# LSTM step on one core: two column groups of the fifth gate ahead of the wait for the state's second half, and an output gate and a tanh that change memories

## The reference

```python
def step(carry, xp):
    h, c = carry
    gates = xp + h @ W_hh.T
    i, f, g, o = jnp.split(gates, 4, axis=-1)
    c = jax.nn.sigmoid(f) * c + jax.nn.sigmoid(i) * jnp.tanh(g)
    h = jax.nn.sigmoid(o) * jnp.tanh(c)
    return ((h, c), h)
_, hs = jax.lax.scan(step, (h0, c0), jnp.swapaxes(x_proj, 0, 1))
```

## Time and profile before

| | us |
|---|---|
| runs | 14405.98, 14417.92, 14417.6 |
| median | 14417.6 |
| span of the profiled execution, first to last instruction | 14425.7 |
| first to last L1510 weight load | 3964.9 to 14307.1 |

### The profile page before, as it was taken

One profiled execution on the slowest core, in us unless ns is written; L12 is line 12 of the kernel. 1 busy time (PEld: TensorE's weight loads), 2 busy tenths in 40 slices (PEclk: granted clock), 3 DMA queues, 4 the chain that ended last, 5 costly groups with the idle time before them and its releaser, 6 DMA issues. The chain is left out here.

```text
span 14425.7 us, 1970254 instructions
## 1 busy us (share of the span) xinstructions
PE 12650.9 (88%) x904808; PEld 11223.3 (78%) x904808; DVE 6842.5 (47%) x48363; ACT 6802.9 (47%) x42405; POOL 2877.4 (20%) x4598
## 2 busy tenths in 40 slices
PE   3697878878699999999999999999999999999998
PEld 2585766756588888888888888888888888888886
DVE  5868677775533333333333333333333333333335
ACT  2474655655144444444444444444444444444443
POOL 5675757667000000000000000000000000000000
PEclk7898998988899999999999999999999999999998
DMA  4454545545200000000000000000000000000000
GB/s 91 128 152 120 148 128 143 136 129 145 94 3 3 2 2 2 3 2 2 2 3 2 2 3 2 2 3 3 2 2 2 3 2 2 3 2 2 3 2 20
DMA packets 692140, 542.16 MB, mean 38 GB/s; under 512 B 545207, under 2 KB 595929, under 8 KB 679740
## 3 DMA queue, kind: packets, MB, share of 16 engines
q1 hardware_dynamic: 469456, 315.98, 8.8%
q0 software_dynamic: 221600, 223.50, 6.6%
q10 hardware_dynamic: 934, 0.99, 0.0%
HBM read 286.02 MB, written 252.14 MB: 37 GB/s over the span
## 5 line engine op out<-in xcount | busy, mean ns | idle before, releaser
L1510 PE MATMUL p_g<-ring,wh 128*32 128x16 f32 x800000 | 8099.8, 185 | 663.2 <-DVE ring L1613 401.0
L1510 PEld LDWEIGHTS p_g<-ring,wh 128*32 128x32 f32 x800000 | 7487.6, 109 | 1438.2 <-DVE ring L1613 1134.2
L1551 ACT ACTIVATE cell<-p_g 128x3 f32<-128x3 f32 x12500 | 2180.9, 174 | 5594.6 <-PE p_g L1510 5594.6
L1606 DVE CUSTOM_DVE_ANT_1 cj<-cell 128x4 f32<-128x4 f32 x12500 | 2038.6, 163 | 5732.3 <-ACT cell L1551 5732.3
L1648 POOL COPY hist<-ring 128x6 f32 x2501 | 475.3, 190 | 10239.6 <-POOLq L1647 10239.6
L426 POOL DMA_INDIRECT eb<-node_tab,eidx x1650 | 2128.2, 1290 | 1013.6 <-POOLq L424 587.6
L1484 PE MATMUL p_g<-xq,idn 128*32 128x24 f32 (+3 forms) x80032 | 1614.8, 189 | 61.6 <-PEq L1497 15.3
L1484 PEld LDWEIGHTS p_g<-xq,idn 128*32 128x32 f32 x80032 | 1254.7, 110 | 231.6 <-issue 15.5
L1613 DVE SCALAR_TENSOR_TENSOR ring<-og,p_g 128x1 f32<-128x1 f32 x6250 | 969.1, 155 | 631.9 <-ACT p_g L1555 1.8
L1555 ACT ACTIVATE tc<-cell 128x1 f32<-128x1 f32 x6250 | 1219.9, 195 | 0.0
L1555 ACT ACTIVATE p_g<-cell 128x1 f32<-128x1 f32 x6250 | 1089.4, 174 | 0.0
(11 more groups left out here) (224 smaller groups left out, 7731.8 us busy)
## 6 DMA issues: line engine op xcount, KB each, us to landing
edge_tab<-eb SPq DMA_DIRECT2D x98, 1019.8 KB
edge_tab<-eb SPq DMA_DIRECT2D x96, 566.6 KB
edge_tab<-eb SPq DMA_DIRECT2D x96, 339.9 KB
eb<-node_tab,eidx POOLq DMA_INDIRECT x1650
xp_tab<-xo SPq DMA_DIRECT2D x50, 500.0 KB, 2.6
xq<-xp_tab SPq DMA_DIRECT2D x1251, 8.0 KB, 1.7
xq<-xp_tab SPq DMA_DIRECT2D x1250, 12.0 KB, 1.7
edge_tab<-eb SPq DMA_DIRECT2D x98, 118.4 KB
```

The costliest lines, as they stand in the source:

```text
L1510: m = pe.matmul(to[32 * q:32 * q + 32], wh[:, k, D * q + 32 * c:D * q + 32 * c + 32], ring[:, (s - 1) % TS, k:k + 1].broadcast_to([128, w] ...
L1551: act.activation(cell[:, s, k, 0:6:2], gate_at(h, u, k)[:, :, 0], ACT.Tanh).then_inc(l_s[k], 1)
L1606: dve.tensor_tensor_reduce(cj[:, k, :].rearrange("p (a b) -> p a b", a=2), cell[:, s, k, 0:4].rearrange("p (a b) -> p a b", a=2), cell[:, ...
```

## The change

Three things: `gate` takes a list of quads, and two of the four groups of column 4 with k = 0 go ahead of the wait for ring's second half; the groups of columns 0 to 2 with k = 1 behind the wait run in the order of quads 2, 3, 0, 1, and the other two groups of column 4 follow them. Half 0's output gate goes to SBUF (`og`, now with an index k), and its tanh of c to PSUM, in scratch columns of bank 0 instead of bank 2. So both halves now have the output gate in SBUF and the tanh in PSUM.

```diff
--- before.py
+++ after.py
@@ -1408,7 +1408,7 @@
                 xq = [sb(sub, f"xq{h}", [128, HB[h], GT]) for h in range(2)]
                 ring = sb(sub, "ring", [128, TS, KC])
                 cell = sb(sub, "cell", [128, TS, KC, 6])
-                og, tc = sb(sub, "og", [128, 2]), sb(sub, "tc", [128, 2])
+                og, tc = sb(sub, "og", [128, KC, 2]), sb(sub, "tc", [128, 2])
                 cj = sb(sub, "cj", [128, KC, 4])
                 part_of = ((0, 3), (3, 6), (6, 7), (7, 8))
                 p_g = [[ps(sub, f"p_g{h}{n}") for n in range(4)] for h in range(2)]
@@ -1440,7 +1440,7 @@
 
                 def late_at(h, u, k):
 
-                    return p_g[h][2 + k][:, 504 + u:505 + u]
+                    return p_g[h][3 * k][:, 504 + u:505 + u]
 
                 @block.sync
                 def _(sp):
@@ -1503,10 +1503,10 @@
                             h, u = place(s)
                             g, v = turn(s)
 
-                            def gate(c, k, w=W):
+                            def gate(c, k, quads=(0, 1, 2, 3), w=W):
                                 n = c // 3 if c < 6 else c - 4
                                 to = gate_at(h, u, n)[:, c - part_of[n][0], 0:w]
-                                for q in range(4):
+                                for q in quads:
                                     m = pe.matmul(to[32 * q:32 * q + 32],
                                                   wh[:, k, D * q + 32 * c:D * q + 32 * c + 32],
                                                   ring[:, (s - 1) % TS, k:k + 1].broadcast_to([128, w]), start=False, stop=(k == KC - 1), skip_group_check=True)
@@ -1514,12 +1514,13 @@
                             pe.wait_ge(l_h[g][0], v)
                             for c in (0, 1, 2, 3):
                                 gate(c, 0)
+                            gate(4, 0, (0, 1))
                             pe.wait_ge(l_h[g][1], v)
                             for c in (0, 1, 2):
-                                m = gate(c, 1)
+                                m = gate(c, 1, (2, 3, 0, 1))
                             m.then_inc(l_g[0], 1)
-                            for c in (4, 5):
-                                gate(c, 0)
+                            gate(4, 0, (2, 3))
+                            gate(5, 0)
                             for c in (3, 4, 5):
                                 m = gate(c, 1)
                             m.then_inc(l_g[1], 1)
@@ -1551,12 +1552,10 @@
                                 act.activation(cell[:, s, k, 0:6:2], gate_at(h, u, k)[:, :, 0], ACT.Tanh).then_inc(l_s[k], 1)
 
                             def tanh_c(k):
-                                to = late_at(h, u, 1) if k else tc[:, s % 2:s % 2 + 1]
-                                return act.activation(to, cell[:, (s + 1) % TS, k, 5:6], ACT.Tanh)
+                                return act.activation(late_at(h, u, k), cell[:, (s + 1) % TS, k, 5:6], ACT.Tanh)
 
                             def out_gate(k):
-                                to = og[:, s % 2:s % 2 + 1] if k else late_at(h, u, 0)
-                                return act.activation(to, gate_at(h, u, 2 + k)[:, :, 0], ACT.Tanh)
+                                return act.activation(og[:, k, s % 2:s % 2 + 1], gate_at(h, u, 2 + k)[:, :, 0], ACT.Tanh)
                             act.wait_ge(l_g[0], s + 1)
                             gates(0)
                             act.wait_ge(l_g[1], s + 1)
@@ -1609,8 +1608,7 @@
                                                          0.5, 0.0, ALU.mult, ALU.add, cell[:, (s + 1) % TS, k, 5:6]).then_inc(l_c[k], 1)
 
                             def new_h(k):
-                                gate, th = (og[:, s % 2:s % 2 + 1], late_at(h, u, 1)) if k else (late_at(h, u, 0), tc[:, s % 2:s % 2 + 1])
-                                dve.scalar_tensor_tensor(ring[:, s, k:k + 1], gate, 1.0, th,
+                                dve.scalar_tensor_tensor(ring[:, s, k:k + 1], og[:, k, s % 2:s % 2 + 1], 1.0, late_at(h, u, k),
                                                          ALU.add, ALU.mult).then_inc(l_h[turn((s + 1) % TS)[0]][k], 1)
                             dve.wait_ge(l_s[0], s + 1)
                             new_c(0)
```

## The result

The changed kernel takes 14537.0 us (median of 4 runs, 14533.4 to 14539.1); the kernel before, in runs on the same chip, 14415.6 us (4 runs, 14406.0 to 14417.9). The ratio is 1.0085, with a 95% interval of 1.0073 to 1.0098: slower by 121 us, where 14555 us and +137 us had been forecast. The profiled execution took 14539.1 us, its span is 14537.3, against 14425.7.

The account below looks back on a forecast made before the run. The first half's loop (TensorE to gates(1), tanh_c(0), out_gate(0), new_h(0), next load) was taken to bound the step. Terms 18 + 8 - 4 = +22 ns over 6250 steps gave 137.5 us, so 14555 us; range 14412 to 14595.

Parts of the forecast that it names:

- The views and the loop: Step of 1.65 us closed by the first half: TensorE to gates(1), then tanh_c(0), out_gate(0), new_h(0), next load.
- Term 5: Second half: gates(1), new_c(1), tanh_c(1) stay in place, new_h(1) stays at 1.70 us and gains slack.
- The wait is free: TensorE's wait for ring's second half opens just as reached and costs nothing; moving two groups ahead fills no hole.
- The stall rival: TensorE idles up to 33 ns at the second-half wait, so the change runs faster: -12 ns a step, 14343 us; 9%.
- Term 1: Two groups moved ahead of l_g0 put gates(0) 33 ns later, at 0.755 us; gates(1) stays at 1.08.
- The rotation at nothing: Rotated group order on TensorE keeps consecutive groups on different columns, so it was costed at zero.
- Term 2: l_c0 opens later, a cover of 15 ns is used up, and tanh_c(0) starts 18 ns late; bounds 10 to 25.
- Term 3: tanh_c(0) to PSUM: the interval to out_gate(0) stays 0.09 us, going with what the first operation reads.
- Term 4: out_gate(0) to SBUF takes 171 instead of 163 ns, +8 on the path; new_h(0) then -4.
- new_h(0) −4: new_h(0) takes the form of new_h(1): 155 instead of 159 ns, -4 a step.
- fixed overlap: ScalarE overlap stays 0.10 us, so out_gate(0) starts 0.072 behind tanh_c(0): 0 to +4 ns, some 14424 us; 18%.
- A write that must land: tanh_c(0)'s PSUM write must finish before out_gate(0) reads PSUM: +103 ns a step, 15060 us; 6%.

Follow-up runs that it names:

- the wait one group earlier: Kernel before, with 15 instead of 16 groups ahead of the wait for ring's second half and the order rotated to match: 14449.4 us, ratio 1.003.
- four groups: Kernel before, with all four groups of gate 4's first pass ahead of the wait, memories as before: 14772.4 us, ratio 1.0244.
- one-group kernel: Kernel before, with one column group of gate 4 instead of two ahead of the wait, memories as before: 14463.4 us, ratio 1.003.
- groups only: Kernel before, with only TensorE's group order as in the change (two groups ahead of the wait, rotated), memories as before: 14562.3 us, ratio 1.0101.
- after: The changed kernel, with both the group order and the two memories changed against the kernel before: 14537.0 us, ratio 1.0085.
- memories only: Kernel before, with only tanh_c(0) moved to PSUM and out_gate(0) to SBUF, TensorE's order as before: 14424.1 us, ratio 1.0004.
- The one run that was to hold tanh_c(0) back: Kernel with four groups ahead of the wait, plus an unread ACTIVATE between gates(1) and tanh_c(0): 14805.2 us, ratio 1.0274.

## Why the prediction was right, and which of its terms were not

The direction, the place and the size held: forecast +22 ns a step and 14555 us, measured +20 and 14537. Point by point:

- *The views and the loop.* Right. The loop of the first half sets the step: in every kernel here the next load stands 53 ns behind new_h(0)'s end (before: 1599.7 and 1652.9). Term 5 holds too: new_h(1) starts at 1700.3, before at 1700.5, and only with the wait one group earlier does the second half hold TensorE by more than it catches up (gates(1) 7.9 ns late).
- *The wait is free.* Right. gates(1) did not move, the burst has the same 38 loads in 0.30 us, and an earlier wait shows about 9 ns of slack. "The wait has next to no slack" was roughly right too, only that a hole of that size is filled again within four loads. The stall rival is refuted.
- *Term 1, 33 ns at gates(0).* Measured 34.0; one, two and four groups give 16.6, 33.3 and 66.6. *The rotation at nothing:* right, and it is worth 17 ns in the run without it.
- *Term 2, +18 ns from a cover of 15.* The start of tanh_c(0) moved by 18.0 (1169.7 against 1151.7), exact as a statement on that start. What it left out is that the cover on the path is not that of tanh_c(0)'s start: out_gate(0)'s start moved by 34.4, its end by 24.4 (1408.1 to 1432.5). The one-group kernel parts the three: 2.4 ns at tanh_c(0)'s start, 18.8 at out_gate(0)'s start, 9 at its end.
- *Term 3, the interval stays 0.09.* Failed: 109 ns, +16. The source of the data, which I took as what decides, is the same in both, and the destination doesn't decide either: 109 with SBUF (groups only) and with PSUM (after), 93 with SBUF (before) and with PSUM (memories only; there the opening + 109 comes to the same time, so this pair says only that it isn't longer). What decides is whether l_c0 or the queue is last. The trace of before held a hint, outside my groups. ScalarE's timeline of the kernel before, at two places where it comes from idling:

```profile
2869.46 0.20 ACT L878 ACTIVATE kf<-kd 128x2 f32<-128x2 f32 x1 [2.21 <-ACTq L877]
2869.57 0.45 ACT L880 ACTIVATE x<-p,kn 128x250 f32<-128x250 f32 x1
...
3535.84 0.21 ACT L1207 ACTIVATE c<-c 125x10 f32<-125x10 f32 x1 [30.90 <-DVE c L1262]
3535.96 0.20 ACT L1208 ACTIVATE c<-c 125x10 f32<-125x10 f32 x1
3536.06 0.39 ACT L1209 ACTIVATE wgt<-mm,cn 125x125 f32<-125x125 f32 x1
```

  The pair whose 0.09 I took as my upper bound stands here again, behind 2.21 us of idle time, and the interval is 0.11. In the second piece the one behind the idle time has 0.12 and its follower 0.10. At both places the interval behind the operation that had to wait is the longer one: 0.11 against the 0.09 of the earlier trace rows, 0.12 against 0.10.
- *Term 4, out_gate(0) 171 instead of 163.* Failed: 154, −10 instead of +8. I took the duration of out_gate(1) for a property of the two memories. Of PSUM to SBUF the runs show 171, 168 and 154 ns, of PSUM to PSUM 164 and 153: it is 153 to 154 with either destination where l_c0 holds it clearly (after, and one, two and four groups). *new_h(0) −4:* right, 155.
- *The two errors cancel.* From the start of tanh_c(0) to the end of out_gate(0) I had 93 + 171 = 264 ns, and it is 109 + 154 = 263. Terms 2, 3, 4 as measured: 18 + 16 − 10 − 4 = +20. That the total came out within 2 ns is luck in these two. The forecast lengthened this way from 256 to 264 for a write to SBUF. As measured, the memories alone take it from 256 to 261, l_c0 alone to 262.5, and both together to 262.8.
- *The halves don't add.* Groups alone cost 144 us, memories alone 6 (not told from none), together 121. Behind an l_c0 that is late, out_gate(0) takes 153 or 154 ns in either memory, so the cost of SBUF for it is gone, and new_h(0)'s 158 to 155 remains as a gain: with the memories the two-group step is 1.6726, without them 1.6752.
- *The rivals.* The fixed overlap is refuted by the result beside the groups alone: behind 174 ns and behind 203 ns out_gate(0) comes 109 later, overlaps of 65 and 94. With the memories alone the overlap is 76, and in the kernel before 102, so no two of these kernels share one. My own reading, that the source sets the interval, was an estimate from a few intervals, and it falls with this one: with tanh_c(0) reading `cell` every time, the interval is 93 or 109 ns. *A write that must land:* refuted, since out_gate(0), which reads PSUM, started 109 and not 174 ns behind a tanh_c(0) that writes PSUM. With the groups alone out_gate(1) stands 123 ns behind an out_gate(0) of 153 ns that writes PSUM (1400.8, 1277.9); it was l_g3 that set its 0.16.

**What stays open.** The rule of the later of two times fits the start of out_gate(0) in every kernel to within 1 ns at the step of the table, and it is a description: why the operation behind the waiting one goes by the opening + 109 is not known, nor why tanh_c(0) takes 8 ns more when l_c0 starts it, and out_gate(0) 10 less behind it. A thread may run through both: with the memories of before, out_gate(0) ends 59 to 62 ns behind tanh_c(0)'s end in every kernel. It is no rule for all, for the changed kernel ends tanh_c(0) 28 ns sooner than the groups alone do (1343.9 and 1371.4), and out_gate(0) not (1432.5 and 1431.1). The one run that was to hold tanh_c(0) back held it for 3 ns. Both late results in PSUM together were not tried.

## What to carry to other kernels

Work moved ahead of one signal and behind another is paid by the first and repaid by none, if the engine between them is paced by its own instructions, as TensorE is here (16.65 ns a group at gates(0) and nothing won at gates(1), with one, two and four groups): count the instructions ahead of each signal, and keep ahead of the one on the loop only what it needs. Measure a cover at the point that the path goes through, here the end of the follower, and not at the operation ahead of it in the queue: the start of the waiting tanh had 16 ns of it, its follower's start none, and its follower's end 10. On a stream paced per instruction, narrow the matmuls that the burst begins with (−62 us here, with 4 columns instead of 16); at the signals it brought nothing (14409.2 us against 14408.5).

## What the runs showed of the hardware that I had not expected

- ScalarE, 128x1 tanh: the one behind an operation with a wait starts 92.5 ns after that one's start or 109 ns after the semaphore's opening, whichever is later (16 ns apart in one direction with the earlier wait, where it starts at 1252.2 and the opening + 109 would be 1235.8; in the other with two groups, where it starts at 1277.9 and the start + 92.5 would be 1261.1, and with four). The start alone says little: in the kernel before, an operation that starts 4 ns later by this rule (96.8 instead of 92.8 behind tanh_c(0)) is 5 ns shorter (159.6 instead of 164.4), and its end stays (256.4 and 257.2). The 109 holds for either destination of the first (after: PSUM; groups only: SBUF); the 92.5 was seen by itself only with SBUF.
- TensorE, once the first 32 loads of a burst are in (in the kernel before the 32nd begins at 234.2, 7.6 ns a load; from the 40th at 317.6 to the 50th at 400.9 it is 8.3), has a spacing of signals of 16.7 ns a group (two loads and two matmuls, 4.17 ns an instruction in the mean) plus 26 ns per signal: the same at 8 and at 16 columns (gates(0) to gates(1) 359.2 in both), and right to 0.6 ns over spacings of 292 to 359 ns.
- The width of the first matmuls counts once per burst (both signals 10.1 ns sooner from 16 to 4 columns), that of the signalling ones not at all (723.3 and 1082.5 with 4 as with 16).
- The same column group again after one other instead of three costs 17 ns a step (gates(0) at 773.5 without the rotation, 756.7 with it), at the first of the two places alone.
- With all matmuls 8 wide instead of 16, the mean granted clock falls in some runs as low as 0.947 of full speed, in the slowest at a cost of 135 us against the fastest.
